# RWKV-6 block with a gated feed-forward on eight cores: four loads of down weights, issued right behind the x0 products from the third tile on

## The reference, cut to what matters

```python
xn = _layernorm(x)                                   # x: 16 x 2048 x 1024
# recurrent part
x5  = tanh((xn + delta * x0_mu) @ x0_w.T)            # delta: previous row - this row
mix = einsum(x5, x2_w) + x_bias                      # five mixes: r, w, k, v, g
r = (xn + delta * r_mu) @ r_w.T                      # k, v, g alike
wv = tanh((xn + delta * w_mu) @ w_w1.T) @ w_w2.T + w_b2
o = chunk_rwkv6(r, k, v, -exp(wv), bonus)            # chunks of 32 rows, 4 heads
s = (group_norm(o) * silu(g)) @ o_w.T
# feed-forward part, integer weights of 8 bits in int32
h = silu(xn @ w_gate.T / 127) * (xn @ w_up.T / 127)  # 3072 wide
f = h @ w_down.T / 127
out = x + s * silu(f)
```

## Time and profile before

| | |
|---|---|
| median of 3 runs | 1717.03 us (1716.47 to 1717.54) |
| the profiled execution's own time | 1717.9 us |
| its span, slowest core (core 6) | 1716.3 us |
| spans of the other cores | 1703.9 to 1715.2 us |
| PE busy on core 6 | 1670.1 us, 97% of the span |
| DVE, ACT, POOL busy | 1086.6, 486.8, 194.5 us |
| granted TensorE clock, mean of a core | 0.994 to 0.998 |
| bytes read from HBM and written to it, a core | 346.82 MB, 44.04 MB |

### The profile page before, as it was taken

The page is one execution under the profiler, slowest core; times in us unless marked ns, Lnnn a source line. Parts: engine busy times, 40 slices in busy tenths (PEclk is TensorE's granted clock), DMA queues, the critical chain, the costliest instruction groups (busy, mean ns, idle before and its releaser), DMA issues.

```text
span 1716.3 us, 26555 instructions; the slowest of 8 cores (1703.9 to 1716.3 us)
## 1 busy us (share of the span) xinstructions
PE 1670.1 (97%) x9252; PEld 777.4 (45%) x9252; DVE 1086.6 (63%) x1844; ACT 486.8 (28%) x815; POOL 194.5 (11%) x408
## 2 busy tenths in 40 slices
PE   5999899999998999999999999999999999999998
PEld 2444444444443454444544445444454445544454
DVE  5565665758656476564875657747576485764756
ACT  3143211442113331133211432115321243212411
POOL 3112301112011020110200001000110001100000
PEclk9999999999999999999999999999999999999999
DMA  9999899997599767997436983466535364354412
GB/s 175 170 167 178 194 229 183 185 172 210 129 178 210 178 209 194 200 218 236 167 114 167 231 286 124 151 179 203 204 123 169 126 233 161 123 184 162 157 65 108
DMA packets 78834, 302.62 MB, mean 176 GB/s; under 512 B 10671, under 2 KB 15088, under 8 KB 73328
## 3 DMA queue, kind: packets, MB, share of 16 engines
q0 software_dynamic: 26912, 94.19, 34.4%
q10 hardware_dynamic: 25488, 124.82, 20.9%
q1 hardware_dynamic: 26304, 81.90, 13.3%
HBM read 346.82 MB, written 44.04 MB: 228 GB/s over the span
## 4 chain that ended last, share of the span: by engine, by line
PE 89%; DMA 6%; DVE 2%; issue 1%; DVEq 1%; POOL 1%; ACT 0%; SPq 0%; POOLq 0%; ACTq 0%
PE PB L1265 20%; PE PB L1270 19%; PE PB L1390 8%; PE PB L1379 8%; PE PB L1543 6%; PE PB L1566 6%; PE PB L1422 6%; PE PB L1488 3%; PE PB L1504 3%; DMA sb_wd<-kept_wd 3%; DMA sb_gu<-w_gu 2%; PE PB L1298 1%; DMA sb_wd<-w_fd 1%; PE PB L1474 1%; PE PB L1453 1%
## 5 line engine op out<-in xcount | busy, mean ns | idle before, releaser
L1265 PE MATMUL PB<-sb_xnT,sb_gu 128*128 128x512 bf16 x1536 | 368.3, 383 | 9.8 <-DMA sb_gu<-w_gu 7.3
L1270 PE MATMUL PB<-sb_xnT,sb_gu 128*128 128x512 bf16 x1536 | 365.3, 381 | 0.0
L944 DVE SCALAR_TENSOR_TENSOR sb_xin<-PB,sb_xb,sb_dT 128x512 bf16<-128x512 f32 x320 | 218.1, 744 | 166.0 <-PE PB L1298 160.3
L698 ACT ACTIVATE sb_scr<-PB 128x512 bf16<-128x512 f32 x192 | 113.8, 597 | 515.1 <-PE PB L1270 495.3
L1270 PEld LDWEIGHTS PB<-sb_xnT,sb_gu 128*128 128x128 bf16 x1536 | 151.2, 98 | 184.0 <-issue 4.9
L1265 PEld LDWEIGHTS PB<-sb_xnT,sb_gu 128*128 128x128 bf16 x1536 | 140.6, 98 | 198.4 <-issue 52.6
L876 DVE SCALAR_TENSOR_TENSOR sb_hall<-PB,sb_scr 128x512 bf16<-128x512 f32 x192 | 130.7, 684 | 117.0 <-ACT sb_scr L698 117.0
L1390 PE MATMUL PB<-sb_wd,sb_hall 128*128 128x512 bf16 x768 | 178.9, 381 | 9.4 <-DMA sb_wd<-w_fd 5.6
L1379 PE MATMUL PB<-sb_wd,sb_hall 128*128 128x512 bf16 x768 | 178.7, 382 | 2.6 <-DMA sb_wd<-kept_wd 2.5
L707 ACT ACTIVATE sb_wc<-PB 128x512 bf16<-128x512 f32 x64 | 38.2, 597 | 322.9 <-PE PB L1390 322.9
L463 POOL DMA_DIRECT2D sb_gu<-w_gu x106 | 57.7, 545 | 622.3 <-PE PB L1270 574.7
(11 more groups left out here) (160 smaller groups left out, 1687.6 us busy)
## 6 DMA issues: line engine op xcount, KB each, us to landing
sb_gu<-w_gu POOLq DMA_DIRECT2D x106, 512.0 KB, 10.7
sb_gu<-kept_gu ACTq DMA_DIRECT2D x86, 512.0 KB, 4.9
sb_wd<-kept_wd ACTq DMA_DIRECT2D x56, 768.0 KB, 7.4
sb_ring<-kept_ring ACTq DMA_DIRECT2D x34, 1024.0 KB, 6.6
sb_xin<-x SPq DMA_DIRECT2D x48, 512.0 KB, 7.3
kept_gu<-sb_gu SPq DMA_DIRECT2D x24, 512.0 KB, 9.2
sb_ring<-w_g POOLq DMA_DIRECT2D x20, 512.0 KB, 16.0
sb_ring<-w_v POOLq DMA_DIRECT2D x16, 512.0 KB, 12.4
```

What stands on the lines that cost most here:

```text
L698: e.activation(out=sb_scr[:, p, :], in_=GB[p][:], func=AF.Silu, bias=0.0, scale=INV127).then_inc(a_silu, 1)
L944: e.scalar_tensor_tensor(out=sb_xin[:, p, c, :], in0=PM[j][:], scalar=sb_xb[:, n, c:c + 1], in1=sb_dT[:, c, :], op0=ALU.add, op1=ALU.mult) ...
L1265: e.matmul(GB[p][:], sb_gu[:, sl, 0, c, :], sb_xnT[:, c, :], start=(c == 0), stop=(c == NC - 1))
L1270: i = e.matmul(UB[p][:], sb_gu[:, sl, 1, c, :], sb_xnT[:, c, :], start=(c == 0), stop=(c == NC - 1))
```

## The change

From tile 2 on, the four loads of the first down half are issued on ACT behind `load_ring(it, 3)`, ahead of `silu_gu(it, 2)`. In tile 1 they stay where they were; in tile 0 they are casts from POOL and untouched. The number and size of the DMAs stay the same, and so do all other instructions.

```diff
                          func=AF.Tanh).then_inc(a_x5, 1)
             load_ring(it, 2)
             load_ring(it, 3)
+            if it > 1:
+                for g in range(4):
+                    load_wd(it, 0, g)
             for hc in range(2, 6):
                 silu_gu(it, hc)
...
             for hc in range(14, 17):
                 silu_gu(it, hc)
-                load_wd(it, 0, hc - 14)
+                if it == 1:
+                    load_wd(it, 0, hc - 14)
             decay_exps(it)
...
                 if half == 0:
-                    load_wd(it, 0, 3)
+                    if it == 1:
+                        load_wd(it, 0, 3)
                     silu_gu(it, 17)
                     silu_gu(it, 18)
```

## The result

The changed kernel takes 1764.53 us (median of 4 runs, 1763.28 to 1764.88) against 1717.28 us: a ratio of 1.0275, 95% interval 1.0263 to 1.0287, 47 us slower. The direction was forecast, the size was not: +16 us had been predicted, with 1746 as the upper end.

What follows compares the result with a forecast made beforehand. The prediction took PE, busy 97% of the span, as the bound, so any new wait adds in full. Waits of 20.6 us plus 7.5 of clock less 12.1 gained gave +16.0, so 1733 us, range 1716 to 1746.

Steps and rivals of the forecast that it cites:

- The end that counts, and the sign: Loads added behind the x0 products make PE wait at units 6 to 8, 20.6 us in sum; slower, chance 0.81.
- The load of unit 6 in tile 6 takes some 17 us: Sign expected in the profile after: this load's time to landing, 8.3 us before, grows to some 17.
- Removed, units 14 to 18: Taking the four loads away there ends the unit 18 stalls of tiles 2 and 3, with their slow matmuls: -12.1 us.
- Four take 8.0 to 9.0 us; I take 8.5: Transfer time of the four 768 KB loads, set ahead of the next unit load in ACT's queue.
- 3.6 us of room: Tile 3, unit 7: free DMA share of 0.36 over 10 us lets 3.6 us of the 8.5 pass at once.
- The queues' turns in tile 4: Unit 6's cast in POOL's queue keeps its pace; only ACT's queue is held: 5.6 us, against some 8 for a common line.
- Tiles 6 and 7: At unit 6, slack of 4.7 us against 8.5 us of added transfer: PE waits 3.8 us in each tile.
- ACT's own time: Four more issues ahead of the silu of unit 2 take 1.6 us, covered by unit 2's 3.46 us: taken as 0.
- SP's copies of x5, put at nothing: SP's 12 copies share the engines but are wanted only behind unit 6; tile 4's smallest margin is covered by unit 7's wait.
- The clock: PE runs slower behind each of five new waits of over 2 us: 1.5 us each, 7.5 in all, ends 0 and 15.
- hidden in the free room: Rival: moved loads slip into engine gaps, PE never waits at unit 6 or 7, only the gain remains: 1705; chance 0.10.
- The dearer rival: Every wait pays 3.0 us of clock and the unit 18 stall stays in tiles 2 and 3: 1747; chance 0.15.

Runs made afterwards that it cites:

- e4: Changed kernel with the same four loads issued from SP's queue behind the x5 copies of v; ratio 1.0104 to the kernel before.
- e5: Changed kernel with the four loads issued on ACT behind the silu of unit 5; ratio 1.0071 to the kernel before.
- e2: The change made in tile 2 alone, loads of the other tiles at their old place; ratio 1.0010 to the kernel before.
- e8: Changed kernel with the cast tables set to 1, so only kept copies are loaded from tile 2 on; ratio 1.0551 to the kernel before.
- e11: Kernel before, with tile 2's four loads and two of tile 3's issued at the end of the tile before; ratio 0.9941 to the kernel before.

## Why the prediction was right or wrong

- *The end that counts, and the sign*: right. PE waits at units 6 and 7 of tiles 3 to 7, the loads stand in line in ACT's queue, and issuing them elsewhere (e4, e5) takes the waits of tiles 4, 6 and 7 at units 6 and 7 away. "The load of unit 6 in tile 6 takes some 17 us" came out as 17.5.
- *Removed, units 14 to 18*: the mechanism was right, the balance of tile 2 wasn't. The stalls at unit 18 went (0.5 us left in tile 2 of core 5, none in tile 3), and the changed kernel's tile 2 waited 3.0 us at unit 8 where 3.9 was forecast. But the sum gave tile 2 a gain of 2.8 us (8.2 less 3.9 and 1.5 of clock), and e2's interval ends at a gain of 1.2. The reason can be read over all cores: PE's waits for casts in tile 2 are 2.0 to 5.2 us before, 3.5 in the mean of the eight, and 1.9 to 4.5 in e2, 3.4 in the mean (traces of two chips). The wait moved and kept its size. The 5.2 of the prediction is core 6, the worst of the eight.
- *The step that failed*: "Four take 8.0 to 9.0 us; I take 8.5", used for every tile. It priced a load by the earlier trace rows, where hardly anything else was in flight. In tile 3, with two more queues at work, a load took 6.0 us and four some 24. My waits of 1.0, 5.6 and 2.5 us for tiles 3, 4 and 5 came out as 10.2, 12.9 and 9.3: 23 us of the 31 missed. I even credited tile 3 with 3.6 us of room, as if free engine time went to ACT's queue alone. The evidence was at hand: the load of unit 7 in tile 4 had taken 10.1 us behind two ring loads, the one in tile 5 7.0. The earlier trace rows even had two of the moved loads themselves at 12.9 us beside the casts, and I read that only as a sign of full engines. The shares of tile 3 and e8 show the cause: ACT's queue had 38.1% of the engines there, so that a load of 2.3 us of engine time took 6.0, and without casts and kept copies beside it all six waits are 4 to 6 us.
- *The queues' turns in tile 4*: I used the rule for one half only. The Trainium skill (DMA: Bandwidth & Descriptors, Queues, rings and completion order) says that an engine takes turns between the queues it has work for. I took from it that the cast of unit 6 keeps its pace, which the run bears out (no wait of PE there); in e4 a load of ACT's queue overtakes an earlier one of SP's, which agrees with it too. So the choice that the prediction called open is settled: no common line. The same rule means that ACT's own queue moves at a share while others have work; the 131 GB/s and the 38.1% of tile 3 agree with that.
- *Tiles 6 and 7*: 3.8 us forecast each, 5.8 and 5.5 measured: 3.7 us of the miss. SP's copies take a share there too (7.6%; 2.6 us a load), and in tile 6 the unit load itself was issued 1.1 us late.
- *ACT's own time*: mis-sized. "1.6 us on four" was 3.1, and in tile 4 3.9, as the timeline of ACT's queue shows; so "covered by unit 2" didn't hold by 1.1 and 1.9 us. It is a side term: its effect is within the waits above.

```profile
898.72 3.86 ACTq L672 DMA_DIRECT2D sb_wd<-kept_wd  x4
...
1342.60 3.12 ACTq L672 DMA_DIRECT2D sb_wd<-kept_wd  x4
```

- *SP's copies of x5, put at nothing*: right. In tile 4 PE waited 1.2 us for one, at 918.74 behind unit 6, and the wait at unit 7 behind it covered that, as forecast.
- *The clock*: 1.5 us a wait was low. The chain gives 6.08, 6.47 and 5.72 us for the units behind the waits of 10.2, 12.9 and 5.8 us, 2.3 to 3.0 over the 3.46 of the earlier trace rows. The five waits for kept weights make 13.2 us in all where I had 7.5, close to my upper end of 15. The wait of 3.0 us in tile 2 cost nothing: its 16 products started at the usual distance.
- *The rivals*: "hidden in the free room" falls for this place, and holds for a place that has the room (e11). The dearer rival named the clock rightly; its other part, a stall that stays at unit 18, didn't come, and its 1747 is still 18 us short, since it too priced the loads at 8.5.

Summed on the slowest cores: new waits 43.7 + 4.1, clock some 13, less 12.1 gained, is 49 us; the spans differ by 46.7.

What stays open: by what rule the engines divide themselves. The shares can be read, but no run changed the casts, the small copies or the kept copies alone.

## What to carry to other kernels

A load that is moved ahead of others in a queue must be priced by the slack of the loads that now stand behind it, at the rate which that queue gets while the other queues are busy, not at the rate of a quiet stretch. Look for a loaded example in the trace at the very place where the load is to go. Free engine time is only worth something if it lies ahead of the moment when the next tightly timed load is issued, and taking part of the load there can be better than taking all of it.

## What the runs showed of the hardware that was not expected

Four DMA issues in a row behind others cost ACT's sequencer 3.1 to 3.9 us, where a single one took 0.33 to 0.41; with no ring loads ahead, in tile 3, the four took 2.5. In one queue a load of 768 KB took 2.0 us in a quiet stretch, 2.6 beside the small copies, and 6.0 beside casts and copies; in the last two cases alike the engines counted as full.

A cast costs far more engine time for its bytes than a plain load. The page after has, for POOL's casting queue:

```profile
q0 software_dynamic: 26912, 94.19, 33.4%
```

That is 33.4% of 1763.0 us for 94.19 MB, 6.3 us per MB, where ACT's queue needs 2.9 (20.6% for 124.82 MB). It fits that full engines move some 250 GB/s in tile 3 and 338 in tile 6.
